# Table products moved ahead of the shared units, last batch's shares spread over them, and TensorE's unread products left out

## The reference

```
x  = input                                     # [4, 512, 256]
sa, ca, ga, sb, cb, gb = split(silu(c) @ wmod) # per sequence; |ga|, |gb| at least 0.25
x += ga * attn(layernorm(x) * (1 + ca) + sa)
h  = layernorm(x) * (1 + cb) + sb
x += gb * (routed(h) + shared(h))

attn:   proj = h @ W_in.T; 4-tap convolution; silu; softplus(dt)
        64 heads of 64, state 128, chunks of 32 tokens:
        masked products within each chunk, gate, rms norm, @ W_out.T
routed: p = softmax(h @ gate_w.T)              # 64 experts
        top 6 of each token, their weights divided by their sum
        y[e] = silu(h @ w1[e].T) @ w2[e].T     # inner size 176
        sum over the six of weight * y[e]
shared: silu(h @ g.T) * (h @ u.T) @ down.T     # inner size 352
```

## Time and profile before

| | us |
|---|---|
| median of 3 runs | 1599.98 |
| lowest, highest | 1594.16, 1605.89 |
| the profiled execution | 1602.16 |
| its span, first to last instruction | 1600.4 |
| PE busy, DVE busy, ACT busy, POOL busy | 1466.4, 1269.3, 966.5, 655.7 |
| mean granted clock of TensorE | 0.956 |
| DMA, mean over the span | 215 GB/s |

### The profile page before, as it was taken

How to read it: one execution, slowest core, us unless ns; L and a number is a source line. 1 busy time by engine, 2 the same in 40 slices (tenths; PEclk the granted TensorE clock), 3 DMA queues, 4 the chain that set the end, 5 groups by cost and what they waited for, 6 DMA issues and landing times.

```text
span 1600.4 us, 29759 instructions
## 1 busy us (share of the span) xinstructions
PE 1466.4 (92%) x9760; PEld 1142.4 (71%) x9760; DVE 1269.3 (79%) x2138; ACT 966.5 (60%) x1729; POOL 655.7 (41%) x554
## 2 busy tenths in 40 slices
PE   5799999799999789999879999976899999999979
PEld 4666676666766576666566667555588999999879
DVE  1788889788899688889969889943468998898854
ACT  3765666657566475656475666542257888888840
POOL 0134344243436624444824344835024554455430
PEclk7999999999999999999989999988869999999999
DMA  4376567466767746667947667812258999998858
GB/s 175 126 227 215 193 201 240 143 220 204 224 201 252 256 147 203 207 213 230 295 136 222 223 219 223 265 42 77 68 167 283 293 295 295 301 301 288 249 199 268
DMA packets 239686, 343.55 MB, mean 215 GB/s; under 512 B 20761, under 2 KB 191399, under 8 KB 238512
## 3 DMA queue, kind: packets, MB, share of 16 engines
q1 hardware_dynamic: 226096, 299.48, 59.2%
q0 software_dynamic: 13440, 42.19, 7.3%
HBM read 177.65 MB, written 172.30 MB: 219 GB/s over the span
## 4 chain that ended last, share of the span: by engine, by line
PE 68%; DVE 16%; issue 6%; ACT 5%; DMA 2%; another core or an unknown queue 1%; SPq 1%; POOL 1%; DVEq 0%; ACTq 0%; POOLq 0%
PE bank L451 13%; PE bank L453 11%; PE bank L452 11%; PE bank L618 11%; PE bank L629 6%; DVE e L1148 4%; PE bank L821 3%; PE bank L605 3%; PE bank L796 2%; PE bank L766 2%; DVE m L1189 2%; ACT e L884 2%; DVE e L1185 1%; DVE xt L1195 1%; DVE el L1161 1%
## 5 line engine op out<-in xcount | busy, mean ns | idle before, releaser
L1546 POOL TENSOR_TENSOR ssq<-ssq,ysq 128x512 f32<-128x512 f32 x128 | 167.9, 1312 | 425.9 <-ACT ysq L955 424.8
L1148 DVE SCALAR_TENSOR_TENSOR e<-bank,scal,e 128x511 f32<-128x511 f32 (+2 forms) x384 | 286.4, 746 | 34.7 <-ACT e L950 25.7
L1629 POOL DMA_INDIRECT outputs<-hsw,x_rows x160 | 182.9, 1143 | 243.2 <-DVE hsw L1492 191.9
L451 PE MATMUL bank<-h_hi,wi_hi 128*128 128x512 f32 x512 | 228.7, 447 | 33.5 <-issue 14.3
L618 PE MATMUL bank<-e,wn 128*128 128x512 f32 x512 | 244.2, 600 | 12.0 <-DVE e L1185 12.0
L1533 POOL TENSOR_TENSOR wi_lo<-wi,wi_hi 128x512 fp32r<-128x512 f32 x128 | 164.9, 1289 | 107.6 <-ACT wi_hi L832 107.6
L452 PE MATMUL bank<-h_lo,wi_hi 128*128 128x512 f32 x512 | 205.8, 402 | 0.0
L453 PE MATMUL bank<-h_hi,wi_lo 128*128 128x512 f32 x512 | 205.7, 402 | 0.0
L950 ACT ACTIVATE e<-bank,scal 128x512 f32<-128x512 f32 x128 | 99.5, 778 | 162.9 <-PE bank L453 160.6
L963 ACT ACTIVATE e<-e 128x512 f32<-128x512 f32 x128 | 80.7, 630 | 172.2 <-DVE e L1148 172.1
L1081 DVE TENSOR_TENSOR ew_lo<-ew,ew_hi 128x864 fp32r<-128x864 f32 x160 | 168.6, 1054 | 15.9 <-ACT ew_hi L832 6.7
(11 more groups left out here) (232 smaller groups left out, 3448.1 us busy)
## 6 DMA issues: line engine op xcount, KB each, us to landing
grouped<-zeros_out SPq DMA_DIRECT2D x256, 520.0 KB
ew<-expert_w SPq DMA_DIRECT2D x160, 432.0 KB
wi<-in_w SPq DMA_DIRECT2D x128, 256.0 KB
x_rows<-grouped SPq DMA_DIRECT2D x160, 130.0 KB
wo<-out_w SPq DMA_DIRECT2D x128, 128.0 KB
got<-outputs SPq DMA_DIRECT2D x16, 768.0 KB, 4.3
seg_wb<-seg_const POOLq DMA_DIRECT2D x4, 2048.0 KB, 8.2
seg_wa<-seg_const POOLq DMA_DIRECT2D x4, 2048.0 KB
```

What stands on the lines that cost most here:

```text
L451: mm(out, w_hi, x_hi, start=first, stop=False)
L1148: v.scalar_tensor_tensor(dst[:, d:], src[:, 0:SEQ - d], taps(TAPS - 1 - d), dst[:, d:], ALU.mult, ALU.add).then_inc(S[done], 1)
L1546: g_.tensor_tensor(ssq[:, :], ssq[:, :], ysq[:, :], ALU.add).then_inc(S["ssq_done"], 1)
L1629: g_.indirect_dma_start(outputs, bass.IndirectOffsetOnAxis(x_rows[:, i % XD, EMB:EMB + 1].bitcast(U32), 0), y_rows[:, i % YD, :], None, bo ...
```

## The change

Three things, all behind the attention.

1. **Tables.** On TensorE the three rounds of table products stand in one piece ahead of unit 4, on DVE the three rounds of table steps stand directly behind the ranks of the fourth batch. `shared_low(3)` and `shared_done(0)` move behind them.
2. **Shares.** The fourth batch's shares are cut into seven pieces: the four opening operations behind unit 4, and one of the six triples behind each of units 5 to 10.
3. **Unread products.** `fill` is gone, with all 184 products (24 + 20 x 8). Waits are as before.

```diff
-PROD_AT, LOW_AT = {8: (0,), 10: (1,), 14: (2,), 21: (3,)}, {10: (0,), 13: (1,), 16: (2,), 24: (3,)}
+PROD_AT, LOW_AT = {8: (0,), 10: (1,), 14: (2,), 21: (3,)}, {10: (0,), 13: (1,), 16: (2,)}
...
+            pe.wait_ge(S["rank_read"], 2 * BATCH)
+            mm(p_count[0:EXPERTS, :], base[:, :], ident[:, 0:8], start=True, stop=True).then_inc(S["count_mm"], 1)
+            pe.wait_ge(S["tiles_done"], 1)
+            mm(p_offset[0:EXPERTS, :], upto_e[0:EXPERTS, :], tiles_row[0:EXPERTS, 0:8],
+               start=True, stop=True).then_inc(S["offset_mm"], 1)
+            pe.wait_ge(S["passed"], 3)
+            pe.wait_ge(S["h_copied"], GTILES)
+            mm(p_owner[:, 0:ETILES], ones[0:EXPERTS, :], passed[0:EXPERTS, :], start=True, stop=True)
+            mm(p_owner[:, ETILES:2 * ETILES], ones[0:EXPERTS, :], row_of[0:EXPERTS, :], start=True, stop=True)\
+                .then_inc(S["owner_mm"], 1)
             for u in range(SPREAD_UNITS, UNITS):
                 inner_shared(u)
                 down_shared(u - 1)
...
-            def fill(times):
-
-                for _ in range(times):
-                    mm(bank[6][:, :], ident_r, h_hi[:, 0, 0:SEQ], start=True, stop=True)
-
             pe.wait_ge(S["result"], BATCH * KE)
             pe.wait_ge(S["weighted"], UNITS)
             pe.wait_ge(S["owners"], 2)
-            fill(24)
             pe.wait_ge(x_in[0], 16)
             turn(0)
             turn(1)
...
                 if i:
                     second(i - 1)
-                if i % 8 == 7:
-                    fill(8)
             second(ETILES - 1)
...
-                if j == ROUTE["rows"]:
-                    shared_done(0)
...
+            tile_counts()
+            tile_places()
+            tile_owners()
+            shared_low(SPREAD_UNITS - 1)
+            shared_done(0)
+            dve.wait_ge(S["attn_res"], BATCH * KE)
             for u in range(SPREAD_UNITS, UNITS):
                 shared_prod(u)
                 shared_low(u)
...
                 if u % SH_CHUNKS == 0:
                     shared_done(u // SH_CHUNKS - 1)
+                k = u - SPREAD_UNITS - 1
+                if k < TOP_K:
+                    share(BATCH - 1, k, k + 1)
             shared_done(BATCH - 1)
-            share(BATCH - 1, -1, TOP_K)
```

More of the change, by code:

```diff
@@ L745, in _ @@
                 down_shared(u - 1)
[L746 to L758, removed]
             down_shared(UNITS - 1)
```

## The result

| | before | after |
|---|---|---|
| median | 1599.98 | 1631.41 |
| executions (5 each) | 1594.16 to 1605.89 | 1617.38, 1623.99, 1631.41, 1676.14, 1716.90 |
| mean granted clock of these | 0.956 (the profiled one) | 0.920, 0.912, 0.910, 0.881, 0.847 |

The change makes the kernel slower by 1.6% (ratio 1.0159, 95% interval 1.0115 to 1.0204). That ratio leaves out the two longest executions as disturbed, though what makes them long is the half clock within the experts that this document is about; the ratio of the medians is 1.0196. The time rises as the mean clock falls, execution by execution. The profile is that of the longest, 1716.90 us, with a span of 1714.7.

What follows compares the result with a forecast made beforehand. TensorE at 1.2 GHz was taken to bound the tiles once the unread products go. From 1602.2 us: shares -9.8, unread products +187.1, tables -3 give 1776.5, or 1774 as median; own range 1756 to 1792, wide range 1600 to 1794.

Steps and rivals of the forecast that it cites:

- The fall at the doorstep: Between last shared unit and first tile: TensorE's clock falls to half in some 3 us with hardly any work.
- Nothing in the experts then brings the clock back, and all 160 tiles run at 3.53 us: Experts: without unread products the clock stays at 1.2 GHz for every tile, first to last copy 561.3 us instead of 374.2.
- rival B: Experts: clock falls at a wait for rows or returns by chance; 1560 to 1755 us; chance 0.09, of which 0.05 slower.
- +187.1: Experts: us added by leaving out the unread products, all tiles at half clock; bounds -3 and +8 on it.
- Rival A: Experts: clock holds or tiles regain it at once, 2.10 us a tile; 1545 us, from 1525 to 1575; chance 0.17.
- Shares: -9.8: Doorstep: shares hide in DVE's idle time, so `ew_lo` moves from 1162.34 to 1152.6; cost at most +9.8, taken as 0.
- Tables: -3: Shared units 4 to 11: table work moved ahead of unit 4 saves 3 us, with bounds of -16 and +4.
- rival C: Shared units: the late semaphores vanish while the clock falls; 1761 us; chance counted within the forecast's 0.74.
- The rule of the Trainium skill: Experts: sustained TensorE activity releases the throttle; prediction set it aside for 26 us busy at half clock, left it a chance.

Runs made afterwards that it cites:

- e7: Changed kernel with groups of 8 unread products after tiles 8, 40, 72, 104 and 136 only; 1572.54 us against 1571.75 for the kernel before on that chip.
- e4: Changed kernel with a single group of 8 unread products, after the eighth tile; 1613.46 us against 1598.42 for the kernel before, ratio of medians 1.009.
- e13: Changed kernel run again unaltered, on another chip; 1622.36 us (1569 to 1663) against 1593.11 for the kernel before, ratio of medians 1.018.
- e1: Changed kernel with all 184 unread products back where they were; 1585.09 us against 1598.42 for the kernel before, ratio 0.9925.
- e12: Changed kernel with one unread product of 512 columns behind every tile, third chip; 1573.92 us against 1598.61 for the kernel before, ratio 0.9847.
- e10: Kernel before with only the fourth batch's shares cut into seven pieces, tables and unread products as before; 1587.89 us against 1598.61, ratio 0.9930.
- e2: Kernel before with only the 184 unread products left out; 1616.04 us (1577 to 1685) against 1598.42, ratio of medians 1.011.
- e9: Changed kernel with one 512-column unread product per tile and the fourth batch's 24 sends issued three at a time; 1559.49 us against 1598.61 before, ratio 0.9743.
- e5: Changed kernel with one unread product of 512 columns behind every tile, second chip; 1552.44 us against 1571.75 for the kernel before, ratio 0.9896.
- e11: Changed kernel with one unread product of 256 columns behind every tile; 1573.98 us against 1598.61 for the kernel before, ratio 0.9856.
- e14: Changed kernel with only the 24 unread products ahead of the first tile back; 1610.60 us (1570 to 1687) against 1593.11 before, ratio of medians 1.011.
- e6: Changed kernel with groups of 4 unread products after every eighth tile; 1556.65 us against 1571.75 for the kernel before, ratio 0.9925.

## Why the prediction was right or wrong

**The fall at the doorstep: right.** The clock is 0.50 from 1152.0, before the first tile. It does not always last, though: in e7, likewise without the 24 products, it was down from 1131.3 to 1134.7 only, and 1.00 again before that kernel's first copy at 1137.2.

**"Nothing in the experts then brings the clock back, and all 160 tiles run at 3.53 us": this step failed.** The pace was right, 155 us of tiles at 0.50 and 3.53 us apart. But the trace of before had shown 26 us of such tiles that did not regain the clock, and I read "not in 26 us" as "never". They do, after 130 to 249 us in the five long stretches, and in e7 it was back after 3.4. I had named this observation as what would refute the forecast, and gave it only 0.09 as rival B.

**+187.1 was mis-sized** for that reason. In the profiled execution it was +124.3, in the median one about 1716.9 - 1631.4 = 85.5 less, so some +39. The 148 us between this estimate and +187.1 are about the whole miss (1774 - 1631 = 143). The price of a low tile is not 3.53 - 2.10 but 3.53 - 2.21 = 1.32 us: in e4 the 152 tiles after the only group lie (1514.9 - 1179.0) / 152 = 2.21 us apart at full clock. From that, the profiled execution had 403 us at 3.53, 114 tiles, which cost 151 us; without them it would have taken about 1566, and the best of e13 took 1568.81.

**Rival A's 1545 was too low**, by the same 0.11 us a tile. It took 2.10, from a pace of 2.05 within a stretch that has groups, and treated the transfers, at 0.88 of their time, as a mere caution. The stretch of e4 after its group:

```profile
1176.00:1514.00 338.00, 313.52 (x3040) 288.82 (x3039) 307.90 (x604) 283.84 (x604) 175.14 (x152) 1.00 0.88 287
```

TensorE is busy for 93% there (98% with the groups), DVE for 91%, and the DMA share is 0.88 as before. Most tiles follow one another at 2.0 to 2.1 us, until a transfer is late, as in the waits of 1.4 to 1.5 us shown above. That the transfers set the 2.21 is read from this, and no run took them away. The 1.82 us of a group were in part hidden in the waits for transfers: 20 of them are 36 us of work, and e1's tiles take 364.6 us, 13 more than 159 x 2.21. One product per tile, the same work, adds nothing to see (1516.5 - 1163.9 = 352.6 us between the first and the last copy in e12, 2.22 a tile). I had priced work by the share of the busiest engine, not by what ends last.

**Rival B is what happened**, in its slower part: falls at a wait for a transfer and returns by chance, 1617 to 1717. It deserved the largest chance. Its condition stood in the profile of before: a wait around 1206 that the clock happened to survive.

**Shares: -9.8 right, and nothing to pay.** `ew_lo` is directly behind the last addition. With the shares alone (e10) the way from the first send to `ew_lo` falls from 1162.34 - 1089.45 = 72.9 us to 63.0, so -9.9. With all products back (e1) the median is 13.3 under before. Its first copy comes only 2.0 us earlier after the first send (78.4 instead of 80.4), since the 24 products now hold TensorE there; the larger gain is in the tiles, 1527.4 - 1162.8 = 364.6 instead of 374.2 between the copies, since in e1 no wait follows the 24 products and the first tiles run at full clock.

**Tables: -3 taken, about 0 found in the times** (e1 against e10), between the bounds of -16 and +4. On the way itself they cost a little: from the first send to the last addition to x it takes 62.8 to 63.1 us in the three profiles with the old order (before, e2, e10), and 64.2 to 65.7 in the eight with the new one on chips where the semaphores come late. In the changed kernel's profile `ew_lo` thus begins 1151.03 - 1085.45 = 65.6 us after the first send. The late semaphores stayed, so rival C did not come true; e9 shows that its mechanism was worth 16 us (the first copy 56.3 instead of 72.4 us after the first send), once the sends are changed and not the tables. The prediction set the late semaphores beside POOL's sends; e5 to e7 show that the sends do not bring them alone.

**The rule of the Trainium skill** ("TensorE: Matmul & The Clock Gate", section "What's actually happening"), that sustained activity releases the throttle, was half right. Tiles do release it, which I had denied; but 155 and 248 us in which the rows show TensorE busy without a hole passed first. Busy by the rows is not enough to count on.

## What to carry to other kernels

Work that nobody reads can be what keeps TensorE's clock: before removing it, ask what brings the clock back after a wait, and take "it did not come back in 26 us" as what it is, 26 us of one trace, and not as "never". A small unread product in every repetition of a loop that waits for transfers anyway cost nothing here and kept the executions within 0.8%; groups 32 tiles apart left them 3% apart. Price such work by the wait that hides it. Where semaphores come late beside a row of indirect transfers, try to pace the transfers, and compare on one chip: the lateness was there on three of the four chips of the experiments.

## What was not expected of the hardware

- 88- to 128-row tiles that keep TensorE busy for 155.00 of 155 us and 248.00 of 248 us stay at 1.2 GHz for that long; with one more product of 256 columns in each, the one low stretch seen ended after 14 us, and six executions lay within 0.8% (e11).
- Waits of TensorE of 1.25 to 1.35 us were followed by half clock within 1.1 us in three profiles (changed kernel, e14, e6). They are three of the ten waits of 1.2 us and more that the sixteen profiles have at full clock between the first and the last copy; the other seven were not followed by a fall, up to 1.36 us in the kernel before. No fall in that stretch came without such a wait.
- Beside 24 indirect sends in a row, 1.3 us apart, eight units of the shared branch took 63 to 66 us on three chips, with one wait of ACT of 18 to 23 us for a finished product, and 47 us on a fourth, without it. With three sends at a time they took 49 us on one of the three, and one wait of 5.8 us was left.
